# Flamingo block, forward, float32: another order of each slot's work on VectorE, ScalarE and GpSimd, one operation fewer for the first norm, another fill

## The reference

```python
def _layernorm(x, axis=-1, eps=1e-05):
    m = jnp.mean(x, axis=axis, keepdims=True)
    v = jnp.var(x, axis=axis, keepdims=True)
    return (x - m) / jnp.sqrt(v + eps)
...
        q = jnp.einsum('bsd,od->bso', query, W) + b
        add_mask = (1.0 - mask.astype(q.dtype)) * NEG
        attn_logits = jnp.einsum('bqd,bkd->bqk', q, memories) + add_mask
        attn_weights = jax.nn.softmax(attn_logits, axis=-1)
        attn_outputs = jnp.einsum('bqk,bkd->bqd', attn_weights, memories)
...
        b_weight = jnp.sign(weight)
        return jnp.einsum('bsi,oi->bso', x, b_weight)
    x = x + jnp.tanh(g_xattn[0]) * _L0_xattn_ref(_layernorm(x, axis=-1), ctx_1024, mask_BxSxS2_ik0, L0_xattn_W, L0_xattn_b)
    x = x + jnp.tanh(g_ffn[0]) * _L0_ffn_ref(_layernorm(x, axis=-1), L0_ffn_weight)
```

## Time and profile before

| | |
|---|---|
| median of 3 runs | 300.28 us (298.22 to 302.97) |
| profiled execution | 300.07 us |
| its span, first to last instruction | 298.0 us |
| mean granted clock of TensorE | 0.989 of 2.4 GHz |
| busy: TensorE, weight loads, VectorE, ScalarE, GpSimd | 95%, 89%, 82%, 74%, 74% |

### The profile page before, as it was taken

The page is one execution under the profiler, slowest core; times in us unless marked ns, Lnnn a source line. Parts: engine busy times, 40 slices in busy tenths (PEclk is TensorE's granted clock), DMA queues, the critical chain, the costliest instruction groups (busy, mean ns, idle before and its releaser), DMA issues.

```text
span 298.0 us, 9189 instructions
## 1 busy us (share of the span) xinstructions
PE 281.8 (95%) x2226; PEld 264.4 (89%) x2226; DVE 245.1 (82%) x752; ACT 221.1 (74%) x649; POOL 220.3 (74%) x529
## 2 busy tenths in 40 slices
PE   7969999999999999999999999999999999999993
PEld 6868989899889899899989998999999999989972
DVE  3776798898698988888889888888888898887683
ACT  3547877887777787788778777887787878778752
POOL 2683778777868877887787778777777787787653
PEclk9979999999999999999999999999999999999998
DMA  6916677778787777887878877787877786771112
GB/s 154 289 41 202 206 229 223 244 235 252 209 246 215 254 224 236 244 247 239 226 249 239 245 239 245 229 233 248 247 226 233 262 249 222 238 239 70 48 62 103
DMA packets 61057, 63.66 MB, mean 214 GB/s; under 512 B 23984, under 2 KB 37360, under 8 KB 61040
## 3 DMA queue, kind: packets, MB, share of 16 engines
q1 hardware_dynamic: 60192, 62.94, 68.6%
q10 hardware_dynamic: 848, 0.53, 0.8%
HBM read 31.98 MB, written 16.78 MB: 164 GB/s over the span
## 4 chain that ended last, share of the span: by engine, by line
PE 50%; POOL 15%; issue 13%; DVE 8%; SPq 6%; DMA 5%; ACT 1%; DVEq 1%; POOLq 1%; ACTq 0%
PE ffn_ps L805 14%; PE pv_ps L725 9%; PE l_ps L774 8%; POOL rstd L302 7%; PE ctx_ps L659 5%; PE x1t_ps L780 5%; DVE st L493 4%; DMA ctx_sq<-in_ctx_dram 4%; PE xt_ps L686 3%; PE pt_ps L716 3%; SPq L240 3%; POOL neg_mask L312 2%; POOL ve L298 1%; DMA x_in<-in_x_dram 1%; DVE x_lo L631 1%
## 5 line engine op out<-in xcount | busy, mean ns | idle before, releaser
L774 PE MATMUL l_ps<-m_sb,x_t 128*128 128x77 f32 x496 | 76.4, 256 | 0.0
L348 POOL TENSOR_TENSOR y<-ffn_scaled,x 128x256 f32<-128x256 f32 x64 | 46.6, 728 | 37.2 <-ACT ffn_scaled L465 30.2
L774 PEld LDWEIGHTS l_ps<-m_sb,x_t 128*128 128x128 f32 x496 | 73.7, 193 | 0.2 <-issue 0.2
L302 POOL TENSOR_TENSOR rstd<-ve,minus_half 128x4 f32<-128x4 f32 (+1 forms) x69 | 67.2, 974 | 5.4
L780 PE MATMUL x1t_ps<-ident,x 128*128 128x128 f32 x256 | 69.5, 275 | 0.0
L725 PE MATMUL pv_ps<-ctx_v,p_t 77*128 77x256 f32 x256 | 67.1, 384 | 0.5 <-ACT p_t L431 0.3
L381 ACT ACTIVATE xs<-x_in,shift,rstd 128x256 f32<-128x256 f32 x62 | 37.3, 601 | 37.1 <-POOL shift L309 36.2
L579 DVE SCALAR_TENSOR_TENSOR x<-pv_ps,recip,x_in 128x256 f32<-128x256 f32 x128 | 55.2, 473 | 0.0
L631 DVE TENSOR_TENSOR x_lo<-x1t_ps,x_hi 128x512 fp32r<-128x512 f32 x64 | 43.2, 675 | 10.0 <-ACT x_hi L476 9.6
L805 PE MATMUL ffn_ps<-wf_t,x_lo 128*128 128x256 f32 x256 | 43.6, 292 | 5.5 <-DVE x_lo L631 4.8
L805 PE MATMUL ffn_ps<-wf_t,x_hi 128*128 128x256 f32 x256 | 47.3, 307 | 1.3 <-ACT x_hi L476 1.3
...
## 6 DMA issues: line engine op xcount, KB each, us to landing
x_in<-in_x_dram SPq DMA_DIRECT2D x64, 256.0 KB, 2.9
out_dram<-y SPq DMA_DIRECT2D x64, 256.0 KB, 2.7
xs_r<-xs SPq DMA_DIRECT2D x56, 256.0 KB, 2.3
...
wq_raw<-in_L_xattn_W_dram ACTq DMA_DIRECT2D x1, 256.0 KB, 4.4
wf_raw<-in_L_ffn_weight_dram ACTq DMA_DIRECT2D x1, 256.0 KB, 8.7
```

The lines of the kernel that those rows point to most:

```text
L302: pool.tensor_tensor(rstd[:, i, kinds], ve[:, i, kinds], minus_half[:, kinds], ALU.pow).then_inc(rstd_done, 1)
L348: pool.tensor_tensor(y[:, i, T - 1], ffn_scaled[:, (r - 3) % 2], x1[:, i, T - 1], ALU.add).then_inc(y_last_done, 1)
L774: ins = pe.matmul(l_ps[:, j * K:(j + 1) * K], x_t[:, r % 2, c, j * P:(j + 1) * P], m_sb[:, c, r % R], start=(c == 0), stop=(c == C - 1))
```

## The change

- GpSimd and ScalarE: `mr1` and `shift1` go. `xs` is now (x - mean) * rstd without the constant 1/16, in `scale_last` in one operation with two per-row operands; ScalarE takes `bias1` = -mean * rstd, one operation of one column on GpSimd. The constant is added where `x_t` is copied out of PSUM: `Copy` becomes `Identity` with a per-row bias there.
- GpSimd's slot: `ve`, `rstd`, `c2`, `bias1`, `xs`, then y(t-3), then the mask. It begins its slots at 2.
- ScalarE's slot: `p_t`, `x_t`, `ffn_scaled`, `x1_hi`, exponentials, `m_sb`, `xs`.
- VectorE's slot: moments, `recip`, logits, y(t-3), `x1_lo`, residual, and the context transpose last.
- Fill: both first masks ahead of the third norm; `wq_c` split over VectorE and ScalarE with a mean in one step per column; `w_ffn` loaded by SyncE; the signs' sum ahead of the first residual, their centring behind it and ahead of moments(4); the four transposes of the signs behind logits(2) instead of ahead of slot 2; `x1_hi`(0) ahead of `x_t`(3); warm-up counts 4, 2 and none become 5, none, 3 and 2.
- The copy `xs_r` is used from sequence 6 on instead of 4.

Definitions of tiles and semaphores, and functions that only wrap lines of before (`stats2`, `low`, `first_sum`, `scaled_ffn`, `high`, `last_sum`) are left out or cut:

```diff
-        MOVE_FIRST = 4
+        MOVE_FIRST = 6
         MOVE_END = NB - 4
...
             load_x(0, 3)
+            sp.dma_start(wf_raw[:], w_ffn.rearrange("(c p) i -> p c i", c=C)).then_inc(wf_loaded, DMA)
+            load_x(0, 4)
             load_mask(0, 2)
-            load_x(0, 4)
...
-            def shift(n, k):
+            def bias(n):
...
                 i = norm1_at(n)
-                pool.tensor_tensor(mr1[:, n % R], st[:, i, 0, :, 1], rstd[:, i, 0], ALU.mult).then_inc(mr1_done, 1)
-                pool.wait_ge(mr1_done, k)
-                pool.tensor_tensor(shift1[:, n % R], one[:], mr1[:, n % R], ALU.subtract).then_inc(shift1_done, 1)
+                pool.tensor_scalar(bias1[:, n % R:n % R + 1], st[:, i, 0, 0:1, 1], -1.0, rstd[:, i, 0, 0:1],
+                                   ALU.mult, ALU.mult).then_inc(bias1_done, 1)
...
+                i = norm1_at(n)
                 j = T - 1
-                pool.tensor_scalar(xs[:, n % R, j], x_in[:, n % N, j], rstd[:, norm1_at(n), 0, j:j + 1],
-                                   shift1[:, n % R, j:j + 1], ALU.mult, ALU.add).then_inc(xs1_done, 1)
+                pool.tensor_scalar(xs[:, n % R, j], x_in[:, n % N, j], st[:, i, 0, j:j + 1, 1],
+                                   rstd[:, i, 0, j:j + 1], ALU.subtract, ALU.mult).then_inc(xs1_done, 1)
...
             norm1(1)
             pool.wait_ge(mask_loaded[0], DMA)
             negmask(0)
-            norm1(2)
-            pool.wait_ge(shift1_done, 3)
-            scale_last(2)
+            negmask(1)
+            norm1_scaled(2)
+            norm1_scaled(3)
+            pool.wait_ge(mask_loaded[1], DMA)
+            pool.wait_ge(logits_done, 1)
+            negmask(2)
+            pool.wait_ge(xt_psum, 1)
+            norm1_scaled(4)
+
...
-                if exists(t0, r + 1):
-                    pool.wait_ge(mask_loaded[(r + 1) % N // 2], landed(t0, r + 1))
-                    at_least(pool, logits_done, t)
-                if exists(t0, r - 3):
...
-                    pool.tensor_tensor(y[:, i, T - 1], ffn_scaled[:, (r - 3) % 2], x1[:, i, T - 1],
-                                       ALU.add).then_inc(y_last_done, 1)
...
+                late = isinstance(t, int) and t == 2
+                if late:
+                    mask_there(t0, r + 1)
                     negmask(r + 1)
+                    pool.wait_ge(gate_ready, 2)
...
-                    shift(r + 3, t + 4)
-                    pool.wait_ge(shift1_done, t + 4)
-                    at_least(pool, xt_psum, t)
+                    pool.wait_ge(xt_psum, t)
                 if exists(t0, r - 2):
                     pool.tensor_tensor(c2[:, (r - 2) % R], rstd[:, r % R, 1], gate_ffn[:],
                                        ALU.mult).then_inc(c2_done, 1)
                 if exists(t0, r + 3):
+                    bias(r + 3)
                     scale_last(r + 3)
-                if isinstance(t, int) and t == 1:
-                    pool.wait_ge(gate_ready, 2)
-
-            pipeline(pool, slot)
+                if exists(t0, r + 1) and not late:
+                    mask_there(t0, r + 1)
+                if exists(t0, r - 3):
+                    last_sum(t0, r - 3)
+                if exists(t0, r + 1) and not late:
+                    negmask(r + 1)
+
+            pipeline(pool, slot, 2)
...
+                act.wait_ge(bias1_done, t0 + n - 1)
...
+                               bias=bias1[:, n % R:n % R + 1]).then_inc(xs0_done, 1)
...
+                act.activation(x_t[:, n, 0], xt_ps[:, 0], ACT.Identity, bias=one[:]).then_inc(xt_done, 1)
...
-            act.dma_start(wf_raw[:], w_ffn.rearrange("(c p) i -> p c i", c=C)).then_inc(wf_loaded, DMA)
...
+            act.wait_ge(wq_mean_done, C)
+            act.activation(wq_c[:, 1], wq_raw[:, 1], ACT.Identity, bias=row_mean[:, 1:2]).then_inc(wq_ready, 1)
             m_step(0, 0, 1)
...
                 act.wait_ge(xt_psum, t0 + n + 1)
                 at_least(act, l_psum, t0 + n - 1)
-                act.activation(x_t[:, n % 2], xt_ps[:], ACT.Copy).then_inc(xt_done, 1)
+                act.activation(x_t[:, n % 2], xt_ps[:], ACT.Identity, bias=one[:]).then_inc(xt_done, 1)
...
+            def scaled_ffn(t0, n):
+                act.wait_ge(c2_done, t0 + n + 1)
...
+                at_least(act, y_last_done, t0 + n - 1)
+                act.activation(ffn_scaled[:, n % 2], ffn_ps[T - 1][:, 0:D], ACT.Copy,
+                               scale=c2[:, n % R, T - 1:T]).then_inc(ffn_scaled_done, 1)
...
+            def high(t0, n):
...
+                act.activation(x1_hi[:, n % 2], x1t_ps[:], ACT.Copy).then_inc(hi_done, 1)
...
             transposed_p(0, 0)
+            transposed_x(0, 2)
             exps(0, 1)
             m_step(0, 1, 3)
-            transposed_x(0, 2)
-            m_step(1, 1, 4)
+            m_step(1, 1, 4, ffn_ps[1])
             scale_rows(0, 3)
-            act.wait_ge(wft_psum, 1)
-            for i in range(C):
-                ins = act.activation(wf_t[:, i], ffn_ps[i][:, 0:D], ACT.Copy)
-            ins.then_inc(wft_ready, 1)
-            scale_rows(0, 4)
...
-                if exists(t0, r - 3):
-                    act.wait_ge(c2_done, t - 2)
-                    act.wait_ge(ffn_psum, t - 2)
-                    at_least(act, y_last_done, t - 4)
-                    act.activation(ffn_scaled[:, (r - 3) % 2], ffn_ps[T - 1][:, 0:D], ACT.Copy,
...
+                second = isinstance(t, int) and t == 2
+                third = isinstance(t, int) and t == 3
                 if exists(t0, r - 1):
                     transposed_p(t0, r - 1)
+                if second:
+                    high(t0, 0)
+                    act.wait_ge(wft_psum, 1)
+                    for i in range(C):
+                        ins = act.activation(wf_t[:, i], ffn_ps[i][:, 0:D], ACT.Copy)
+                    ins.then_inc(wft_ready, 1)
                 if r % 2 == 0 and exists(t0, r + 2) and not squares(t0, r + 2):
                     keys_step((r // 2 + 1) % 2, 3 if t < 4 else 4)
+                if second:
+                    scale_rows(t0, 4)
                 if exists(t0, r + 1):
                     transposed_x(t0, r + 1)
-                if exists(t0, r - 2):
-                    act.wait_ge(x1t_psum, t - 1)
-                    at_least(act, ffn_psum, t - 3)
-                    act.activation(x1_hi[:, r % 2], x1t_ps[:], ACT.Copy).then_inc(hi_done, 1)
+                if third:
+                    high(t0, 1)
+                if exists(t0, r - 3):
+                    scaled_ffn(t0, r - 3)
+                if exists(t0, r - 2) and not second and not third:
+                    high(t0, r - 2)
+                if third:
+                    scale_rows(t0, 5)
                 if exists(t0, r):
                     exps(t0, r)
                 if r % 2 == 0 and exists(t0, r + 2):
                     m_step(0, (r // 2 + 1) % 2, t + 3)
                 if r % 2 == 1 and exists(t0, r + 1):
                     m_step(1, (r // 2 + 1) % 2, t + 3)
-                if exists(t0, r + 3):
+                if exists(t0, r + 3) and not second:
                     scale_rows(t0, r + 3)
...
-                at_least(dve, mr1_done, t0 + n - 3)
+                at_least(dve, xs1_done, t0 + n - 3)
...
-            ins.then_inc(wq_ready, 1)
+                dve.tensor_scalar(row_mean[:, c:c + 1], row_sum[:, c:c + 1], bq_col[:, c:c + 1], -1.0 / D,
+                                  ALU.subtract, ALU.mult).then_inc(wq_mean_done, 1)
+            dve.wait_ge(wq_mean_done, C)
+            dve.tensor_scalar(wq_c[:, 0], wq_raw[:, 0], row_mean[:, 0:1], None, ALU.add).then_inc(wq_ready, 1)
...
             stats1(0, 3)
             logits_there(1)
-            prob_recip(0, 0)
             logits(1)
             signs_step = signs()
+            prob_recip(0, 0)
+            sums_step = sign_sums(signs_step)
             residual1(0, 0)
+            centred_signs(sums_step)
             stats1(0, 4)
-            dve.wait_ge(prep_step, signs_step)
-            centred_signs()
-            stats1(0, 5)
...
-                if exists(t0, r - 3):
-                    i = (r - 3) % R
-                    dve.wait_ge(ffn_psum, t - 2)
-                    dve.wait_ge(c2_done, t - 2)
-                    if exists(t0, r - 7):
-                        dve.wait_ge(y_stored[i], landed(t0, r - 7, R))
-                    for j in range(T - 1):
...
-                    ins.then_inc(y_done, 1)
-                if exists(t0, r - 2):
-                    dve.wait_ge(x1_done, t - 1)
-                    at_least(dve, ve_done, t)
-                    moments(x1, (r - 2) % R, norm2_at(r - 2), 1, stats2_done)
-                if exists(t0, r + 4):
+                late = isinstance(t, int) and t == 2
+                if exists(t0, r - 2) and not late:
+                    stats2(t0, r - 2)
+                if exists(t0, r + 4) and not late:
                     stats1(t0, r + 4)
                 if exists(t0, r):
```

(75 more changed lines are left out.)

49 lines of the change are left out of this document (26 added, 23 removed).

## The result

The changed kernel takes 302.92 us in the median of 20 runs, the one before 300.77 in 20 of its own. The ratio is 1.0063, 95% interval 1.0036 to 1.0091: slower by 0.6%, where 286 was forecast. Some executions of each kernel fall into a second, slower state: medians here take all executions, ratios the fast ones alone. The profiled execution has 302.96 us and a span of 301.1, 3.1 more than before.

The account below looks back on a forecast made before the run. A ring of GpSimd and ScalarE, 4.27 us per slot, was taken as the bound. Slots at 4.04 + 0.05 + 0.04 = 4.13 gain 10.3, the fill 3.7: 300.07 - 10.3 - 3.7 = 286.1, so 286 us; range 280.5 to 293.

Parts of the forecast that it names:

- part 1: GpSimd and ScalarE: new orders open their ring; GpSimd's turn becomes 3.5 us, under TensorE's 4.04; 15.3 us to gain.
- part 3: SyncE's queue: the store waiting for a later y delays the copy `xs_r` and x_in; 0.04 us added per slot.
- second rival: SyncE, over two slots: store waiting for y delays copies, odd copy 0.9 us late, slot 4.28, 294 us; chance 0.12.
- third rival: Same SyncE path, y slipping behind the next slot's norms: odd copy 1.8 us late, slot 4.54, 309 us; chance 0.04.
- The ring: GpSimd and ScalarE, steady slots: `shift1`, `xs`, `ffn_scaled`, y, mask, norms, next `shift1` wait in a circle, 4.27 us per slot.
- TensorE's floor of 4.04: Steady slots: a slot in which TensorE waits for nothing takes 4.04 us, the next bound once GpSimd and ScalarE are freed.
- `x_t`'s operand at 0.09: ScalarE's copy `x_t`: the added per-row bias lengthens it by 0.09 us.
- The wait for `x_lo` of 0.05: TensorE's second half product: waits 0 to 0.1 us for VectorE's `x1_lo`, taken as 0.05 per slot.
- The fill: Before the steady slots: `p_t` of slot 3 at 22.6 instead of 26.74, 4.1 us gained, taken as 3.7.
- What would show it: Signs: `p_t` to `p_t` 4.1 us, no `xs` waits for GpSimd; slots at 4.27 with ScalarE busy would refute part 1.

Follow-up runs that it names:

- fast_form: Changed kernel with GpSimd's half of `xs` again as mult, add, from a bias made in two steps; all orders stay new: ratio 0.9778, 295.8 us.
- Both repairs together: Changed kernel with `xs` as mult, add and the store of y(t-4) instead of y(t-3), in two placings: 284.0 and 284.6 us.
- old_order: `fast_form` with GpSimd, ScalarE and VectorE in the old orders from slot 4 on: ratio 0.9901, 298.3 us.
- old_pool: `fast_form` with GpSimd's order alone the old one from slot 4 on: 348.4 us in its one run.
- fast_store_late: `fast_form` with SyncE's store of y(t-4), replacing y(t-3), behind the copy `xs_r` and ahead of the loads: ratio 0.9434, 284.0 us.
- fast_store_end: `fast_form` with the store of y(t-4), replacing y(t-3), at the end of SyncE's slot, behind the loads: ratio 0.9411, 284.6 us.
- fast_store_act: `fast_form` with the store of y(t-4) issued by ScalarE behind `p_t` instead of by SyncE: ratio 0.9868, 297.0 us.
- store_late: Changed kernel, slow `xs` kept, with SyncE's store of y(t-4), replacing y(t-3), behind the copy `xs_r`: ratio 0.9776, 294.9 us.

## Why the prediction was wrong

The failed step is in part 1: "I estimate 0.27 and 0.63 from the start distances of `mr1` and y and the halved width", with the sum "which leaves 3.5" for GpSimd's turn. I priced `xs` by its old form and didn't price the subtraction. Part 1 priced the new bias between two bounds; the edit beside it, a large operation with another pair of operations, it carried over at its old cost. It measured 1.23, 0.67 more. GpSimd's turn became 4.22 instead of 3.5, and passed TensorE's 4.04. The rest of the difference is small: the bias took 0.26 where 0.2 was reckoned, and the sum for the old turn, 3.8, was 0.1 short: it left out `shift1`'s own 0.28, and took `c2` and `xs` 0.17 too long together.

The second failed step is the term of part 3, "so I add 0.04 per slot". The mechanism stands in the text, in part 3 and as the second and third rivals: the store ahead of the copy, decided by when y ends. Its size was wrong, and not only because of the slow form: `fast_form` has the fast one, and its slots came to 4.32 (4.27 settled), where 0.04 was added to 4.09. For the third rival, with a chance of 0.04, the argument against it was "GpSimd has 0.5 us of slack per slot"; this came from the same wrong price, and GpSimd had no slack.

Both repairs together give 284.0 and 284.6, near the forecast of 286. In the changed kernel the form and the store are worth 18 to 19 us together (302.9 less 284.6 or 284.0), and each repair alone gives 7 to 8. These differences are between chips; by the ratios to the kernel before on the same chip they are 19 to 20 and 8.6.

Point by point:

- The ring bounds the kernel before: right. `old_order` brings its wait back, `old_pool` lengthens it as computed.
- TensorE's floor of 4.04 is next: right, `fast_store_late` and `fast_store_end` sit on it.
- `x_t`'s operand at 0.09: right, 0.673 against 0.582. The wait for `x_lo` of 0.05: the waits of the changed kernel and of the repaired ones have no such line from 100 to 250 us, but `fast_store_act` shows how near it is: there 0.27 more on ScalarE brings it, 0.18 a slot.
- The fill: right. `pt` of slot 3 was forecast for 22.1 and `p_t` for 22.6, and `p_t` is at 22.61. The block from 18.2, at 0.55 of the clock in the earlier trace rows, now runs at full clock: the pause of 2.08 ahead of it is gone, and the longest that TensorE stands idle from 9 to 18 us is 0.58. Windows of the changed kernel, columns as in the earlier trace rows:

```profile
18.20:22.00 3.80, 3.80 (x32) 3.65 (x31) 3.70 (x12) 3.54 (x11) 3.28 (x7) 1.00 0.15 56
```

- What would show it: "If `xs_r` or x_in heads the waits, part 3 was priced too low" came true. The sign named for a failure of part 1 was a busy ScalarE; none was named for GpSimd.
- The range of 280.5 to 293 left the measured time out. Its second rival, at 294, and its third, at 309, both stood on TensorE's floor of 4.04, because GpSimd's own turn never entered the bounds.

**Open.** The slots 3 to 17 are slower than the rest in every kernel but `old_pool`: 4.80 against 4.32 settled in the changed one, 4.40 against 4.29 before, 4.49 against 4.27 in `fast_form`, 4.43 against 4.26 in `store_late`, 4.23 against 4.06 in `fast_store_late`. Each repair takes 0.3 to 0.4 off them and both together 0.57, so form and store act there too, and more strongly than later. TensorE waits in that stretch for `xs_r` and VectorE for x_in, up to 1.8 us at once. Most of what the changed kernel loses against the one before, 5.6 of 6.9 us, lies there, so the cause of that part is shown only as far as the repairs remove it. Single issues of SyncE are long in that stretch (1.46 us for a mask at 48.02 and for x_in at 79.99, where 0.35 to 0.6 are usual); why, and why the transfers land late there, wasn't tried.
